# Local attention on one Trainium2 core: TensorE and ACT take the steps of a tile in another order

## The reference, cut to what matters

```
for i in range(6):
    x = attn_layer(shift_tokens(x), ...) + x
    x = ffn_layer(shift_tokens(x), ...) + x

attn_layer:  q, k, v = split(x @ Wqkv)                    # 16 heads of 64
             q, k = l2norm(q) * qs, l2norm(k) * ks         # then rotary, with a scale
             sim = 8 * q k^T, over windows of 32 rows,     # each sees its own window
                   masked                                  # and the one before it
             out = softmax(sim) v
             return out @ Wo
ffn_layer:   xn = layernorm(x) * g + b
             a, gate = split(xn @ W1 + b1)
             return a * gelu(gate) @ W2 + b2
```

## Time and profile before

| | |
|---|---|
| runs | 5449.53, 5436.67, 5445.46 us; median 5445.46 |
| profiled execution | 5438.05 us, of it the span of the trace 5436.3 us |
| mean granted TensorE clock | 0.940 |
| busy, share of the span | PE 87%, PEld 56%, DVE 76%, ACT 62%, POOL 50% |
| instructions | 135547 |

### The profile page before, as it was taken

The page is one execution under the profiler, slowest core; times in us unless marked ns, Lnnn a source line. Parts: engine busy times, 40 slices in busy tenths (PEclk is TensorE's granted clock), DMA queues, the critical chain, the costliest instruction groups (busy, mean ns, idle before and its releaser), DMA issues. The chain is left out here.

```text
span 5436.3 us, 135547 instructions
## 1 busy us (share of the span) xinstructions
PE 4737.4 (87%) x51446; PEld 3032.6 (56%) x51638; DVE 4133.6 (76%) x8982; ACT 3352.3 (62%) x7201; POOL 2735.3 (50%) x3646
## 2 busy tenths in 40 slices
PE   4775899999999999777777778658999999999997
PEld 2232566666666666434444344335666666666665
DVE  5897677777777777479898999966777777777774
ACT  2432677777777777444545444435777777777775
POOL 1221666666666666223233333316666666666663
PEclk7898999999999999988888889869999999999999
DMA  0000222222222222100000000002222223222221
GB/s 18 0 0 12 75 71 71 68 69 69 78 62 74 67 76 63 27 15 2 2 2 2 1 2 2 2 1 79 67 73 65 77 62 79 65 74 67 76 63 40
DMA packets 162491, 247.18 MB, mean 45 GB/s; under 512 B 36228, under 2 KB 56640, under 8 KB 161734
## 3 DMA queue, kind: packets, MB, share of 16 engines
q1 hardware_dynamic: 161862, 238.65, 16.9%
HBM read 36.15 MB, written 1.05 MB: 7 GB/s over the span
## 5 line engine op out<-in xcount | busy, mean ns | idle before, releaser
L940 POOL TENSOR_TENSOR f_rope<-f_rope,f_t 128x1024 f32<-128x1024 f32 x384 | 905.7, 2359 | 524.2 <-DVE f_t L854 524.2
L953 POOL TENSOR_TENSOR f_rope<-f_rope,f_rn 128x1024 f32<-128x1024 f32 x384 | 730.6, 1903 | 56.7 <-POOL f_rn L932 2.6
L490 PE MATMUL psum<-f_wqkv,f_xs 128*128 128x512 f32 x1536 | 729.6, 598 | 22.6 <-DVE f_t L854 22.6
L859 DVE TENSOR_REDUCE f_ss<-f_sq 128x16 f32<-128x1024 f32 x384 | 459.9, 1198 | 335.9 <-ACT f_sq L721 333.0
L1827 POOL TENSOR_SCALAR tk_scores<-tk_scores,tk_m 128x408 f32<-128x408 f32 (+28 forms) x232 | 239.2, 1031 | 783.2 <-DVE tk_m L1787 619.3
L684 ACT ACTIVATE f_kT<-psum 64x512 f32<-64x512 f32 (+1 forms) x960 | 485.3, 525 | 83.4 <-PE psum L481 73.8
L721 ACT ACTIVATE f_sq<-psum 128x1024 f32<-128x1024 f32 x384 | 393.3, 1024 | 218.7 <-PE psum L490 218.3
L854 DVE TENSOR_TENSOR f_t<-psum,f_rot 128x1024 f32<-128x1024 f32 x384 | 466.0, 1213 | 0.0
L850 DVE TENSOR_TENSOR f_rope<-psum,f_rot 128x1024 f32<-128x1024 f32 x384 | 465.3, 1212 | 0.0
L876 DVE TENSOR_REDUCE f_den<-f_prob 128x16 f32<-128x1024 f32 x192 | 234.2, 1220 | 296.0 <-ACT f_prob L726 296.0
L490 PEld LDWEIGHTS psum<-f_wqkv,f_xs 128*128 128x128 f32 x1536 | 279.3, 192 | 305.9 <-issue 298.7
(11 more groups left out here) (240 smaller groups left out, 9759.7 us busy)
## 6 DMA issues: line engine op xcount, KB each, us to landing
f_v<-f_v_tok SPq DMA_DIRECT2D x1152, 128.0 KB, 2.4
f_v<-f_v_tok SPq DMA_DIRECT2D x768, 64.0 KB, 2.0
f_wqkv<-in_Wqkv SPq DMA_DIRECT2D x36, 512.0 KB, 4.0
f_wo<-in_Wo SPq DMA_DIRECT2D x12, 512.0 KB, 4.0
f_w<-in_W SPq DMA_DIRECT2D x12, 341.0 KB, 3.3
f_w<-in_W SPq DMA_DIRECT2D x24, 64.0 KB
tk_wkv<-in_Wkv SPq DMA_DIRECT2D x1, 1024.0 KB
out<-y_tok SPq DMA_DIRECT2D x4, 256.0 KB, 2.5
```

Source lines behind the costliest of these rows:

```text
L490: last = pe.matmul(psum[:, n, :], xs[:, j % 2, :], wqkv[:, INNER * which + 512 * n:INNER * which + 512 * (n + 1)], start=True, stop=True)
L859: dve.tensor_reduce(ss[:, H * half:H * (half + 1)], sq[:, half, :, :], AX_X, ALU.add).then_inc(s[f"{name}_ss"], 1)
L940: pool.tensor_tensor(part, part, t2[:, half, :, :], ALU.add).then_inc(s[f"{name}_added"], 1)
L953: pool.tensor_tensor(part, part, rn[:, H * half:H * (half + 1)].unsqueeze(2).to_broadcast([P, H, DH]), ALU.mult).then_inc(s[f"{name}_norme ...
```

## The change: what it does

In TensorE's step the keys are turned directly behind their tile's projections, ahead of the feed-forward piece, and the probabilities behind it; the output product comes ahead of the weighing, and the turning and the projection of the queries come behind the weighing. In the step j = 2 with a feed-forward the second gated piece comes ahead of the weighing and the third right behind it; the queries, the output product and the scores follow. The waits for banks 2 and 3 follow the new order: the keys wait for the result's copies, the probabilities for the keys' copies, the queries for the probabilities' copies. In ACT's step the copies of the keys come ahead of the even values and the first gelu, those of the probabilities behind them, and the third gelu with the table load moves up behind the second. DVE, GpSimd and SP are unchanged.

```
--- before.py
+++ after.py
@@ -572,25 +572,30 @@
         if on(g, 2):
             wait(pe, "exp_done", through(g, 2))
             for n in range(2):
+                if on(g, 1):
+                    wait(pe, f"kt{n}_evac", through(g, 1))
+                else:
+                    wait(pe, f"ot{n}_evac", through(g, 3))
+                turn(T0 + n, prob, 8 * n, f"pt{n}_full")
+
+    def turn_keys():
+        if on(g, 1):
+            wait(pe, "k_normed", through(g, 1))
+            for n in range(2):
                 if on(g, 3):
                     wait(pe, f"ot{n}_evac", through(g, 3))
                 else:
                     wait(pe, f"qt{n}_evac", through(g, 2))
-                turn(T0 + n, prob, 8 * n, f"pt{n}_full")
-
-    def turn_keys():
-        if on(g, 1):
-            wait(pe, "k_normed", through(g, 1))
-            for n in range(2):
-                if on(g, 2):
-                    wait(pe, f"pt{n}_evac", through(g, 2))
                 turn(T0 + n, rope[:, (j - 1) % 2, 1, :, :], 8 * n, f"kt{n}_full")
 
     def turn_queries():
         if on(g, 1):
             wait(pe, "q_normed", through(g, 1))
             for n in range(2):
-                wait(pe, f"kt{n}_evac", through(g, 1))
+                if on(g, 2):
+                    wait(pe, f"pt{n}_evac", through(g, 2))
+                else:
+                    wait(pe, f"kt{n}_evac", through(g, 1))
                 turn(T0 + n, rope[:, (j - 1) % 2, 0, :, :], 8 * n, f"qt{n}_full")
 
     def weigh():
@@ -650,23 +655,25 @@
 
     values()
     keys()
-    turn_prob()
+    turn_keys()
     if f is not None and j == 2:
         gated(0)
     else:
         feed({0: "mean", 1: "wide", 3: "out"}.get(j))
-    turn_keys()
-    weigh()
+    turn_prob()
     if f is not None and j == 2:
         gated(1)
-    turn_queries()
-    queries()
-    if f is not None and j == 2:
+        weigh()
         gated(2)
+        turn_queries()
+        queries()
+        output()
         score()
-        output()
     else:
         output()
+        weigh()
+        turn_queries()
+        queries()
         score()
         if j == 0:
             feed("var")
@@ -741,15 +748,6 @@
     square(1, "k")
     if j == 2:
         evacuate(1)
-    if on(g, 2):
-        wait(act, "pv_done", through(g, 3))
-        for n in range(2):
-            wait(act, f"pt{n}_full", through(g, 2))
-            copy(flat4(probT, n), psum[:, T0 + n, :]).then_inc(s[f"pt{n}_evac"], 1)
-    if j != 2:
-        evacuate(0)
-    if f is not None and j == 2:
-        gelu(0)
     if on(g, 1):
         sj = (j - 1) % 4
         slot = WIN + P * (sj % 2)
@@ -764,8 +762,20 @@
                     copy(kT[rows, 4 * n:4 * n + 4, par, 0:WIN], turned[rows, :, P - WIN:P])
                 last = copy(kT[rows, 4 * n:4 * n + 4, par, slot:slot + P], turned[rows, :, :])
             last.then_inc(s[f"kt{n}_evac"], 1)
+    if j != 2:
+        evacuate(0)
+    if f is not None and j == 2:
+        gelu(0)
+    if on(g, 2):
+        wait(act, "pv_done", through(g, 3))
+        for n in range(2):
+            wait(act, f"pt{n}_full", through(g, 2))
+            copy(flat4(probT, n), psum[:, T0 + n, :]).then_inc(s[f"pt{n}_evac"], 1)
     if f is not None and j == 2:
         gelu(1)
+    if f is not None and j == 2:
+        gelu(2)
+        act.preload_act_table_set(EXP_LN)
     if j != 2 and on(g, 0):
         inverse("k", 1, g + 1)
     if on(g, 1):
@@ -782,9 +792,6 @@
     if f is not None and j == 1:
         wait(act, "ff_scaled", f + 1)
         act.activation(xn[:, :], xn[:, :], ACT.Identity, bias=layer_vec(k.ln_b, ff[0]), scale=layer_vec(k.ln_g, ff[0])).then_inc(s["ff_gained"], 1)
-    if f is not None and j == 2:
-        gelu(2)
-        act.preload_act_table_set(EXP_LN)
     if j == 2 and on(g, 0):
         inverse("k", 1, g + 1)
     if on(g, 3):
```

More of the change, by code:

```diff
@@ L574, in turn_prob @@
                             for n in range(2):
-                                if on(g, 3):
+                                if on(g, 1):
+                                    wait(pe, f"kt{n}_evac", through(g, 1))
+                                else:
                                     wait(pe, f"ot{n}_evac", through(g, 3))
-                                else:
-                                    wait(pe, f"qt{n}_evac", through(g, 2))
                                 turn(T0 + n, prob, 8 * n, f"pt{n}_full")
@@ L584, in turn_keys @@
                             for n in range(2):
-                                if on(g, 2):
-                                    wait(pe, f"pt{n}_evac", through(g, 2))
+                                if on(g, 3):
+                                    wait(pe, f"ot{n}_evac", through(g, 3))
+                                else:
+                                    wait(pe, f"qt{n}_evac", through(g, 2))
                                 turn(T0 + n, rope[:, (j - 1) % 2, 1, :, :], 8 * n, f"kt{n}_full")
```

## The result

The changed kernel takes 5997.23 us (median of 4 runs, 5995.4 to 6001.41) where the kernel before takes 5442.56 in the same measurement: a ratio of 1.1014 with a 95% interval of 1.1001 to 1.1027, slower by some 555 us. The forecast was 6085 with a range of 5830 to 6220. The profiled execution has a span of 5994.0 us and a mean granted clock of 0.921 (before 5436.3 and 0.940).

A forecast was written before the change was run, and what follows sets the result against it. TensorE's own instructions were taken to bound the kernel before, a closed loop through ACT, DVE and TensorE the changed one. 5438 + 456 (loop) + 192 (clock falls) = 6086, stated as 6085 us, range 5830 to 6220.

The forecast's parts named there:

- TensorE bounds the kernel before, the helpers just keep up: In both stacks TensorE, busy 199.38 of 200 us, sets the time; the helpers' chain is as long as the work hiding it.
- The closed loop: Chain through DVE, ACT and TensorE, from queries' end to queries' end: 18.7, 18.7, 22.8, 19.7 us, 79.9 a group against 70.33.
- The step from tile 2 to 3: Transition forecast as bound by TensorE, 19.7 us, with the key copies just in time behind the feed-forward output.
- The term of +456 us: Cost of the longer loop without clock falls: 9.5 us charged to each of all 48 groups in both stacks.
- What in the change costs: Output product moved ahead of weighing, from behind the query projection, where it gave squares, DVE's chain and exponent 2.0 us cover.
- SP's queue: Ten DMAs per step spreading the values after the weighing: hidden with 0.4 us to spare; 1 us later would cost 58 us.
- The gelu in tile 2: Second gate product waits from 13.4 to 14.8 us after the zero for ACT's table load (1.28) and first gelu (0.69).
- The clock's term: Falls of TensorE's granted clock after waits: one in each of three stalled steps per group, +192 us, bounds 0 and 383.
- The price of a fall: Time lost on TensorE per clock fall, taken from the earlier trace: 1.33 us over eight transposes and the weighing.
- The count: Number of clock falls forecast: one in each of the three stalled steps of a group, for 48 groups.
- The example in the Trainium skill: Taken by its 3 to 5 us waits, the forecast waits bring no clock fall: 5894 us, as the rival with chance 0.23.

The follow-up runs named there:

- the kernel with filled waits: Changed kernel plus unread products of constants on TensorE in its waits (tile 0, gated step, steps without a feed-forward): 5899.33 us, ratio 1.0835 to the kernel before.
- the kernel without the table load: Changed kernel with the identity in the place of the gelu, so no ACT table load ahead of it: 5852.44 us, ratio 1.0742 to the kernel before.

## Why the prediction was right, step by step

*TensorE bounds the kernel before, the helpers just keep up.* Right: an extra 0.63 us of ACT per step is free before and not after. That DVE's part of the chain is on the loop too is read from the timeline; no experiment lengthened it.

*The closed loop.* Right in mechanism and size. Its marks in tile 0 agree within 0.2 us, its four steps within 0.4, and the group's sum was 79.9 against a measured 79.55. The step from tile 2 to 3, which I had put down to TensorE, grew by 0.64 as well with the copy added on ACT, so ACT is level with TensorE there. The term of +456 us is what the kernel with filled waits shows (455). That the two agree to 1 us is luck: a group with a feed-forward cost 9.2 us and not 9.5, one without cost 11, in part for the clock, and the 17 us of the emptying pipelines were not in the sum.

*What in the change costs.* Wrong in one sentence. I wrote that moving the output product in front of the weighing is what costs. Undone alone it returned some 25 us. In the changed order the loop is set by the row on ACT (exponent, key square, key copies) between DVE's subtraction and the probability transposes; without the output product in front, the weighing waits for ACT's probability copies instead. Only in the order before, where no key copies lie in that row, does the move cost 190 us by itself.

*SP's queue.* Hidden, as said, but with 0.1 us of room instead of 0.4. It was the first thing to bind as soon as ACT's order was changed.

*The gelu in tile 2.* Right: a wait of 1.34 forecast as 1.4, gone with the table load. The wait for the odd values' copy (1.06) lies ahead of it and was not named; it cost nothing more, since the key copies behind it were late anyway.

*The clock's term* is the one that was mis-sized, and most of the gap between 6085 and 5997: 192 us forecast, 98 measured by filling the waits, or some 117 with the 19 estimated for the steps without a feed-forward. The price of a fall was low (1.4 to 2.0 us in tile 0, 1.4 to 3.1 in tile 2, against 1.33). The count was wrong: three per group forecast; in 22 groups 16 fell in tile 0, none in tile 1 and 12 in tile 2. In tile 1 the widening splits the wait, 1.16 and 0.50 instead of 1.74 and 0.50. I had written that the feed-forward pieces only fill the waiting; here it moves part of it, and no clock was lost. I had also misread the row that gave the price: the wait of 1.50 us in the earlier trace rows was followed by eight transposes at full speed, and the slow ones stood behind a second wait, of 0.88 us in the same rows. The step that didn't fall had 0.40 there:

```profile
590.30 1.06 PE L481 MATMUL psum<-ident,f_rope 128*128 128x128 f32 x8 [0.40 <-ACT f_probT L684]
```

The example in the Trainium skill, "TensorE: Matmul & The Clock Gate", section "HAM oscillation — how this bites in real kernels", with its waits of 3 to 5 us and each burst at the half clock behind them, fits this kernel only in part: in the groups with a feed-forward the clock fell where no single wait was longer than 1.9 us, and in some steps but not in others of the same form.

Left open: why one wait brings the fall and the same wait a group later does not. In tile 2 the waits are 1.06, 0.37, 0.83 and 1.34 in steps with a fall and without. In the kernel without the table load tile 0 has the same waits as the changed one and hardly falls. With the output product back, tile 1 fell behind waits of 0.58, 0.50 and 0.99 (mean 19.4 to 19.8, shortest 18.4), while tile 0 with 0.61, 0.50 and 0.99 hardly did (3 of 22). The runs show that more work on TensorE prevents it and that the falls follow neither the longest single wait nor the sum of waits of a step; what they follow I did not separate.

## What to carry to other kernels

An order that keeps one engine at 99% can hide a second loop that is just as long: before moving a step, follow one such loop once around, through every engine's own queue, and write down where each part is covered. Moves on one loop need not add up, so price them together and test each alone. A cheap test of whether an engine has room is one extra instruction at the place in question: here it cost nothing in one order and all of itself in the other.

## What the runs showed of the hardware that was not expected

- More matmuls made the kernel faster: products that nobody reads, 2.74 us of them in the waits of each tile 0 and five in each tile 2, took 98 us off; the granted clock of the shown stretch is 1.00 instead of 0.97.
- A fall can last through two pieces of work: in tile 2 the weighing behind the second gate pair still took 3.13 us instead of 1.95.
- A change in one step (1.29 us less in tile 2) took away falls of the clock in another step (tile 0) whose own waits had not changed.
